# Routing seven groups ahead of the last, group-wise one-hot tables, a multiply on GpSimd and a gate column of its own, in a gated cross-attention and mixture-of-experts block

## The reference

```python
# x: 4 x 1024 x 256; ctx: 4 x 77 x 256; mask: 1 x 1024 x 77
x = x + tanh(g_xattn[0]) * xattn(layernorm(x), ctx, ctx, mask, W1, b1, W2, b2)   # softmax attention over 77 keys
h = layernorm(x).reshape(4096, 256)
route   = softmax(h @ router_w + router_b)          # 8 experts
max_ind = argmax(route); max_prob = max(route)
for e in range(8):                                   # only the chosen expert's y counts
    a, g = split(h @ w1[e])                          # 256 -> 2 x 1024
    y = silu(a) * g @ w2[e]                          # 1024 -> 256
    out = where(max_ind == e, y, out)
x = x + tanh(g_ffn[0]) * out * max_prob
```

## Time and profile before

| | us |
|---|---|
| median of 3 runs | 452.51 |
| lowest, highest | 451.57, 454.33 |
| the profiled execution | 450.66 |
| its span (first to last instruction) | 448.6 |

### The profile page before, as it was taken

One profiled execution on the slowest core, in us unless ns is written; L12 is line 12 of the kernel. 1 busy time (PEld: TensorE's weight loads), 2 busy tenths in 40 slices (PEclk: granted clock), 3 DMA queues, 4 the chain that ended last, 5 costly groups with the idle time before them and its releaser, 6 DMA issues.

```text
span 448.6 us, 9824 instructions
## 1 busy us (share of the span) xinstructions
PE 399.7 (89%) x2431; PEld 346.0 (77%) x2432; DVE 213.7 (48%) x520; ACT 175.9 (39%) x337; POOL 246.2 (55%) x323
## 2 busy tenths in 40 slices
PE   5998872149999999999999999999999999999990
PEld 4887751037888888888888888888888888888880
DVE  4888995842443443344443444433434434444340
ACT  1276650014543454545532344445433543233230
POOL 2566989020875677887773258728852676232221
PEclk9999996558999999999999999999999999999997
DMA  7951222652333044433342103433331011001010
GB/s 212 361 188 51 97 99 80 102 200 84 119 118 117 23 147 173 145 117 117 123 161 80 36 18 117 135 112 124 117 117 36 4 36 36 24 24 28 24 35 11
DMA packets 29850, 44.27 MB, mean 99 GB/s; under 512 B 8377, under 2 KB 25581, under 8 KB 27791
## 3 DMA queue, kind: packets, MB, share of 16 engines
q1 hardware_dynamic: 24095, 34.58, 23.4%
q0 software_dynamic: 3456, 9.24, 6.3%
q10 hardware_dynamic: 2288, 0.33, 0.5%
HBM read 35.57 MB, written 8.96 MB: 99 GB/s over the span
## 4 chain that ended last, share of the span: by engine, by line
PE 79%; POOL 8%; DVE 6%; DMA 2%; issue 2%; ACT 1%; DVEq 0%; SPq 0%; POOLq 0%; ACTq 0%
PE py L1093 22%; PE pa L1075 22%; PE pg L1075 21%; PE ph L1085 7%; POOL w_lo L411 2%; PE px L1060 2%; POOL rstd L395 2%; PE ps_s L1004 1%; DMA ctx_in<-in_ctx 1%; POOL slot_iota L432 1%; PE ps_p L948 1%; DMA x_sorted<-residual_rows,idx_gather 1%; DVE x_all L728 1%; PE ps_xt L920 1%; POOL mask_c L387 1%
## 5 line engine op out<-in xcount | busy, mean ns | idle before, releaser
L875 DVE TENSOR_TENSOR ht_lo<-ph,ht_hi 128x512 fp32r<-128x512 f32 x70 | 48.4, 692 | 135.9 <-ACT ht_hi L610 135.9
L481 POOL TENSOR_TENSOR w_lo<-staging,w_hi x84 | 107.4, 1307 | 6.7 <-ACT w_hi L631 4.0
L610 ACT CAST ht_hi<-ph 128x512 fp32r<-128x512 f32 x70 | 41.1, 587 | 121.3 <-PE ph L1085 86.0
L1093 PE MATMUL py<-w_hi,ht_hi 128*128 x280 | 81.3, 290 | 0.8 <-DVE out_tile L883 0.8
L1093 PE MATMUL py<-w_hi,ht_lo 128*128 x280 | 78.4, 280 | 0.0
L1093 PE MATMUL py<-w_lo,ht_hi 128*128 x280 | 78.3, 280 | 0.0
L470 POOL DMA_INDIRECT out<-out_tile,idx_now x34 | 34.7, 1019 | 72.0 <-DVE out_tile L883 71.3
L1075 PE MATMUL pa<-w_hi,xt_hi 128*128 (+1 forms) x140 | 58.8, 420 | 0.8 <-ACT xt_hi L592 0.8
L439 POOL DMA_INDIRECT x_sorted<-residual_rows,idx_now x34 | 35.6, 1048 | 40.8 <-DVE x_norm L858 22.7
L1075 PE MATMUL pg<-w_hi,xt_hi 128*128 (+1 forms) x140 | 56.1, 401 | 0.0
L1075 PE MATMUL pa<-w_lo,xt_hi 128*128 (+1 forms) x140 | 56.1, 401 | 0.0
(11 more groups left out here) (167 smaller groups left out, 577.5 us busy)
## 6 DMA issues: line engine op xcount, KB each, us to landing
staging<-in_L_ffn_w SPq DMA_DIRECT2D x24, 1024.0 KB, 4.9
residual_rows<-x_all SPq DMA_DIRECT2D x8, 532.0 KB, 3.6
x_all<-in_x SPq DMA_DIRECT2D x8, 512.0 KB, 9.9
x_sorted<-residual_rows,idx_now POOLq DMA_INDIRECT x34, 3.9
out<-out_tile,idx_now POOLq DMA_INDIRECT x34, 2.5
w_in<-in_L_xattn_W SPq DMA_DIRECT2D x2, 256.0 KB, 4.7
ctx_in<-in_ctx SPq DMA_DIRECT2D x1, 308.0 KB
mask_in<-in_fside_1xSxS ACTq DMA_DIRECT2D x1, 308.0 KB, 11.2
```

What stands on the lines that cost most here:

```text
L481: lo = nc.gpsimd.tensor_tensor(out=w_lo[:, bass.ds(dst + q * QW, QW)], in0=staging[:, bass.ds(src + q * QW, QW)], in1=w_hi[:, bass.ds(dst ...
L610: nc.scalar.copy(ht_hi[:, j], ph[j][:]).then_inc(hhi_ready[j], 1)
L875: nc.vector.tensor_tensor(out=ht_lo[:, j], in0=ph[j][:], in1=ht_hi[:, j].bitcast(FP32), op=ALU.subtract).then_inc(hlo_ready[j], 1)
L1093: last = mm(py[:, 0:D], ht[:, j, c * P:(c + 1) * P], w[:, bass.ds(slot + (DC * PW + (j * HC + c) * D), D)], start=j == 0 and n == 0, stop= ...
```

## The change

Five edits.

1. `norm2` makes the logits before it writes the two numbers of the row.
2. The routing up to `onehot` runs twice (`PARTS`): for the 28 tiles of groups 0 to 6, and for the 4 tiles of group 7. ACT's exponential is split likewise. The gates and all that follows run once, when both are done.
3. The tables shrink to one group's width (128 x 4 and 55 x 4), and the comparisons read them again for each group. `slot_hot` and `col_hot` are laid out by group, with a group's 4 tiles innermost. The one-hots are made in three rounds (`ROUNDS`) of 3, 3 and 2 groups, `col_hot` ahead of `slot_hot`; `FIRST` goes from 3 to 4, as the tables now reach into group 3, and DVE no longer waits for the other row stores.
4. The product with the token's number is made by POOL for the first round (a semaphore each way), by DVE for the others.
5. A row becomes mean x rstd, rstd, the 256 values and the gate (259 numbers instead of 266); the gate has its own column, so SP stores gates without waiting for the row stores. POOL waits for the row stores ahead of the first gather instead.

```diff
-    ROW = XW + 2
+    X0 = 2
+    XROW = X0 + XW
+    KEPT = X0 + D
+    ROW = KEPT + 1
-    HT = NT // 2
-    FIRST = 3
+    PARTS = ((0, NG - 1), (NG - 1, NG))
+    ROUNDS = ((0, 3), (3, 6), (6, NG))
+    FIRST = 4
...
-        slot_iota = sb1("slot_iota", [P, P, NT], FP16)
-        col_iota = sb1("col_iota", [P, COLS, NT], FP16)
-        slot_hot = sb1("slot_hot", [P, P, NT], FP16)
-        col_hot = sb1("col_hot", [P, COLS, NT], FP16)
+        slot_hot = sb1("slot_hot", [P, NG, P, B], FP16)
+        col_hot = sb1("col_hot", [P, NG, COLS, B], FP16)
+        slot_iota = sb1("slot_iota", [P, P, B], FP16)
+        col_iota = sb1("col_iota", [P, COLS, B], FP16)
...
# SP
             for g in range(NG):
                 sp.wait_ge(rstd2_ready, g + 1)
-                sp.dma_start(rows_groups[g], x_all[:, g]).then_inc(first_stored if g < FIRST else rows_stored, 16)
-            sp.wait_ge(first_stored, 16 * FIRST)
-            sp.wait_ge(rows_stored, 16 * (NG - FIRST))
+                sp.dma_start(rows_groups[g, :, :, 0:KEPT], x_all[:, g, :, 0:KEPT]).then_inc(first_stored if g < FIRST else rows_stored, 16)
             sp.wait_ge(gate_ready, 1)
...
# POOL, norm2
-                nc.gpsimd.tensor_copy(x_all[:, g, :, XW + 1], rstd2[:, g])
-                nc.gpsimd.tensor_tensor(out=x_all[:, g, :, XW], in0=mv2[:, r, :, 0], in1=rstd2[:, g],
-                                        op=ALU.mult).then_inc(rstd2_ready, 1)
...
                                         op=ALU.add).then_inc(logits_ready, 1)
+                nc.gpsimd.tensor_copy(x_all[:, g, :, 1], rstd2[:, g])
+                nc.gpsimd.tensor_tensor(out=x_all[:, g, :, 0], in0=mv2[:, r, :, 0], in1=rstd2[:, g],
+                                        op=ALU.mult).then_inc(rstd2_ready, 1)
...
+            end_group = ROUNDS[0][1]
+            pool.wait_ge(col_ready, 1)
+            nc.gpsimd.tensor_tensor(out=col_hot[:, 0:end_group], in0=col_hot[:, 0:end_group],
+                                    in1=token_of[:, 0:end_group].unsqueeze(2).to_broadcast([P, end_group, COLS, B]),
+                                    op=ALU.mult).then_inc(token_ready, 1)
+
+            pool.wait_ge(first_stored, 16 * FIRST)
+            pool.wait_ge(rows_stored, 16 * (NG - FIRST))
             pool.wait_ge(gate_stored, 16 * B)
             pool.wait_ge(lists_ready, 1)
...
# DVE, routing
-            dve.wait_ge(logits_ready, NG)
             dve.wait_ge(consts_ready, 4)
...
+            for part, (first_group, end_group) in enumerate(PARTS):
+                at = slice(first_group * B, end_group * B)
+                n = (end_group - first_group) * B
+                dve.wait_ge(logits_ready, end_group)
+                link(nc.vector.tensor_reduce(best[:, at], logits[:, at], AX.X, ALU.max))
...
+                nc.vector.tensor_tensor(out=onehot[:, :, at], in0=expert_m8[:].unsqueeze(2).to_broadcast([P, E, n]),
+                                        in1=first[:, at].unsqueeze(1).to_broadcast([P, E, n]),
+                                        op=ALU.is_equal).then_inc(onehot_ready, 1)
+            dve.wait_ge(onehot_ready, len(PARTS))
+            dve.wait_ge(gate_exp, len(PARTS))
...
# DVE, one-hots
             dve.wait_ge(first_stored, 16 * FIRST)
-            dve.wait_ge(rows_stored, 16 * (NG - FIRST))
...
+            for r, (first_group, end_group) in enumerate(ROUNDS):
...
+                nc.vector.tensor_tensor(out=col_hot[:, at], in0=of_group(col_iota, COLS),
+                                        in1=of_token(pos_f[:, 0], COLS), op=ALU.is_equal).then_inc(col_ready, 1)
+                slots = nc.vector.tensor_tensor(out=slot_hot[:, at], in0=of_group(slot_iota, P),
+                                                in1=of_token(pos_f[:, 1], P), op=ALU.is_equal)
+                if r == 0:
+                    slots.then_inc(hot_ready, 1)
+                else:
+                    dve.wait_ge(col_ready, r + 1)
+                    nc.vector.tensor_tensor(out=col_hot[:, at], in0=col_hot[:, at], in1=of_token(token_v[:], COLS),
+                                            op=ALU.mult).then_inc(hot_ready, 1)
...
# PE
+            for r, (first_group, end_group) in enumerate(ROUNDS):
+                if r == 0:
+                    pe.wait_ge(token_ready, 1)
+                pe.wait_ge(hot_ready, r + 1)
+                for g in range(first_group, end_group):
+                    for b in range(B):
+                        last = mm(ps_s[0][:, 0:COLS], slot_hot[:, g, :, b], col_hot[:, g, :, b],
+                                  start=g == 0 and b == 0, stop=g == NG - 1 and b == B - 1)
```

More of the change, by code:

```diff
@@ L575, in _ @@
                     high0(i)
-            act.wait_ge(centered, 1)
-            nc.scalar.activation(work_e[:], work_b[:], ACT.Exp).then_inc(gate_exp, 1)
+            for part, (first_group, end_group) in enumerate(PARTS):
+                at = slice(first_group * B, end_group * B)
+                act.wait_ge(centered, part + 1)
+                nc.scalar.activation(work_e[:, at], work_b[:, at], ACT.Exp).then_inc(gate_exp, 1)
             act.wait_ge(tab_psum, 1)
@@ L645, in stats1 @@
                 for b in range(B):
-                    last = nc.vector.bn_stats(bn1[:, g, b], x_all[:, g, b, 0:D])
+                    last = nc.vector.bn_stats(bn1[:, g, b], x_all[:, g, b, X0:KEPT])
                 last.then_inc(bn1_ready, 1)
@@ L735, in stats2 @@
                 for b in range(B):
[L736 removed]
+                    last = nc.vector.bn_stats(bn2[:, r, b], x_all[:, g, b, X0:KEPT])
                 last.then_inc(bn2_ready, 1)
@@ L777, in _ @@
[L777 to L783, removed]
@@ L784, in _ @@
-            dve.wait_ge(gate_exp, 1)
+            dve.wait_ge(consts_ready, 4)
+            for part, (first_group, end_group) in enumerate(PARTS):
+                at = slice(first_group * B, end_group * B)
+                n = (end_group - first_group) * B
+                dve.wait_ge(logits_ready, end_group)
+                link(nc.vector.tensor_reduce(best[:, at], logits[:, at], AX.X, ALU.max))
+                nc.vector.tensor_tensor(out=work_b[:, at], in0=logits[:, at],
+                                        in1=best[:, at].unsqueeze(2).to_broadcast([P, n, E]),
+                                        op=ALU.subtract).then_inc(centered, 1)
+                dve.wait_ge(centered, part + 1)
+                link(nc.vector.scalar_tensor_tensor(out=work_a[:, at], in0=work_b[:, at], scalar=0.0,
+                                                    in1=expert_m8[:].unsqueeze(1).to_broadcast([P, n, E]),
+                                                    op0=ALU.is_equal, op1=ALU.mult))
+                link(nc.vector.tensor_reduce(first[:, at], work_a[:, at], AX.X, ALU.min))
+                nc.vector.tensor_tensor(out=onehot[:, :, at], in0=expert_m8[:].unsqueeze(2).to_broadcast([P, E, n]),
+                                        in1=first[:, at].unsqueeze(1).to_broadcast([P, E, n]),
+                                        op=ALU.is_equal).then_inc(onehot_ready, 1)
@@ L815, in _, with of_group, of_token @@
             dve.wait_ge(first_stored, 16 * FIRST)
-            dve.wait_ge(rows_stored, 16 * (NG - FIRST))
[L817 to L828, removed]
+            for r, (first_group, end_group) in enumerate(ROUNDS):
+                at = slice(first_group, end_group)
+                n = end_group - first_group
+                def of_group(table, m):
+                    return table[:].unsqueeze(1).to_broadcast([P, n, m, B])
+                def of_token(v, m):
+                    return v.rearrange("p (g b) -> p g b", b=B)[:, at].unsqueeze(2).to_broadcast([P, n, m, B])
+                nc.vector.tensor_tensor(out=col_hot[:, at], in0=of_group(col_iota, COLS),
[8 more added lines that the diff above has]
+                                            op=ALU.mult).then_inc(hot_ready, 1)
             dve.wait_ge(lists_step, 1)
@@ L919, in transpose_tokens @@
                     for b in range(B):
-                        last = nc.tensor.transpose(ps_xt[k][:, b * P:(b + 1) * P], x_all[:, g, b, k * P:(k + 1) * P],
+                        last = nc.tensor.transpose(ps_xt[k][:, b * P:(b + 1) * P], x_all[:, g, b, X0 + k * P:X0 + (k + 1) * P],
                                                    ident[:])
```

39 lines of the change are left out of this document (15 added, 24 removed).

## The result

The changed kernel took 449.33 us in the median of 18 runs (447.0 to 452.5), the kernel before 452.19 in 18 runs beside it (450.6 to 455.55). The ratio is 0.9934, 95% interval 0.9909 to 0.996: 3.0 us less (1.8 to 4.1). The prediction was 449.3, in a range of 446.9 to 451.3. A second series (8 and 25 runs) gave 0.9901 (0.9862 to 0.994).

The account below looks back on a forecast made before the run. TensorE bounds the loop, which can only start earlier. A gain of 3.6 us before the one-hots less 0.3 there, taken as 3.2, gave 450.66 - 3.2 = 447.4; the median lies 1.85 above: 449.3, range 446.9 to 451.3.

Parts of the forecast that it names:

- The one-hots: Comparisons, products and list matmuls: VectorE held by POOL's 1.6 us product, matmuls at 0.123 us each; a loss of 0.3 us.
- a step put at nothing: First gather: comes earlier along with SP's weight loads, its length changed only by 3% through shorter rows.
- The tables and the lateness of POOL: Before the routing: smaller tables take 0.83 us, covered by 4.8 us until group 7's statistics, so POOL is no longer late.
- Seven groups first: Routing up to onehot: part 0 hides behind norm2(7), part 1 takes 1.13 us; onehot is complete 3.84 us earlier.
- term of 0.2 us for collisions: Routing part 0 beside norm2(7): POOL's short operations hold DVE up by 0.2 us, between bounds of 0 and 1.1.
- Rival B: In norm2(7), POOL's power function also holds DVE: 1.0 us less, gain 2.2, 450.3 us; chance 0.11.
- From O to T: From onehot complete to the first comparison of the one-hots: the 5.06 us in between stay unchanged.
- Rival A: One-hots: DVE and POOL don't exclude each other; stage gains 0.7 us, 448.0 us in all; chance 0.22.
- D: One-hots: POOL's product is slow; at 4.9 us the whole gain is gone, at 9.4 the time is 457; chance 0.09.
- What costs nothing: Gate stores, row stores, moved waits, weight loads, shorter rows: nothing lost; gates land by 86.3, with 4.4 us of cover.
- The clock: Start of the loop: full clock back near 101 us, with the first up matmul at 97.0; before, 4.2 us after it.
- rival C: Start of the loop: the clock rises at the same moment as before, 104.4; gain 1.6 us, 450.9 us; chance 0.08.

Follow-up runs that it names:

- one-part kernel: Changed kernel with all 32 tiles routed in one part instead of seven groups ahead; 450.64 us, ratio 0.9935 to the kernel before.
- same kernel with quarters: Changed kernel with all products on VectorE, rounds of 4, 3 and 1 groups, GpSimd's weight subtractions in quarters, not eighths; 449.39 us, ratio 0.9919 to the kernel before.

## Why the prediction was right

The direction was right, and the first two steps for the reason given. The time came out to 0.03 us, and that is luck: the one-hots gained 1.06 us more than forecast, the first gather took 0.2 to 1.8 back, a step put at nothing, and the interval of the measured gain alone is 2.3 us wide.

**The tables and the lateness of POOL.** Right: POOL waits 1.77 us for group 7's statistics instead of being 2.5 late, and S to O is 3.50 for a predicted 3.46 (3.26 and 0.2 of charge). Wrong in its price: the tables took 1.21 and 0.58 us, 2.4 and 2.6 ns a number and not 1.0. It stayed hidden, but not under the 4.8 us of cover that I counted: `norm2(6)`, 2.27 us, lies in them, and 1.77 were left. And the 7.09 us that this step starts from belong to one execution; the second profile of before has 6.56, against which the step gains 0.5 less.

**Seven groups first.** The term of 0.2 us for collisions was right in sum and wrong in its side. I had DVE wait for POOL; DVE's operations took their 0.39, and POOL was held, its power function 1.19 and the next 0.40. The logits came at S + 2.39 instead of 2.06, and DVE, done with part 0, waited 0.46. The one-part kernel shows the 0.31 us as what DVE's presence costs. Rival B, a power function that holds DVE for 1.0, is out: an operation with two inputs in SBUF, begun at 77.53, ran in 0.39 us inside POOL's power function (77.19 to 78.38).

**From O to T.** Missed by 0.12: DVE now waits for `onehot` to be complete where it ran on before.

**The one-hots.** The mechanism was right: POOL's product got its turn right after the slot comparison and held the next comparison, 1.59 us for 0.50. Rival A is out. Mis-sized were two terms. The product was taken as 1.6 us in working time; alone it takes 1.29, and between DVE's operations 1.15 (from the slot comparison's end at 86.85). The matmuls were left at 0.123 each; they take 0.068, as the layout by group brings their numbers together. A loss of 0.33 was forecast, 0.71 was gained (6.73 to 6.02). Of the 1.06 between, 0.46 is the product (DVE is done at T + 5.36 and not 5.82) and 0.60 the matmuls. I named faster matmuls only under rival A, and there for the weights, which make the smaller part; they belonged into the forecast with a chance of their own. D, a slow product, did not come: 2.0 ns a number.

**What costs nothing.** Right for the gates (the run with SP's waits back); the waits of POOL and the row format were not varied by themselves. Wrong for the first gather: I wrote that the loads come earlier "with the gather" and left its 3.61 us as it stood. It took 3.99 and 5.34 in the two profiles of the changed kernel, 3.61 and 3.85 before. So L to U gave back 0.2 to 1.8 us. The 1.06 us that the one-hots gained beyond the forecast went there, in part or in whole.

**The clock.** The sum took it to come back at the same distance from the first up matmul, 4.2 us. In the first profile of the changed kernel that was 3.75 us (at 102.5), in the second 5.9, and in the second of before 5.9 as well; over the 14 profiles it is 2.9 to 5.9, at 100.3 to 107.5. So neither the forecast's fixed distance nor rival C's fixed moment holds; what sets it isn't shown, and it alone moves the time by up to 1.4 us (half of 3.0, roughly). The granted clock by stretch in the changed kernel (from:to, length, busy us of PE, PEld, DVE, ACT, POOL, clock, DMA):

```profile
99.00:102.00 3.00, 3.00 (x8) 2.35 (x9) 0.06 (x1) 0.90 (x1) 0.36 (x1) 0.50 0.51 128
102.00:103.00 1.00, 1.00 (x5) 0.82 (x4) 0.00 (x0) 0.00 (x0) 0.00 (x0) 0.78 1.07 376
103.00:106.00 3.00, 3.00 (x14) 2.42 (x14) 1.01 (x2) 0.89 (x2) 0.10 (x1) 1.00 0.41 143
```

**The account of the two first profiles.** The spans differ by 0.9 us (448.6, 447.7). S came 2.26 later; 1.59 of that the second profile of before has too, and variants with the change lie at 74.5 to 75.0. S to U gained 3.77. The third `x_norm` cost 1.27 more, which also occurs before (1.99 in its second profile); the earlier clock and the rest give back 0.66. The forecast of 3.2 for the change is to be set against 3.77 and, with the long gather, 2.2 to 2.4 in the stretch, and 3.0 (1.8 to 4.1) in the medians.

## What to carry to other kernels

Shrink what stands in front of a late engine before splitting the work behind it: small tables, read again by an access pattern, gave 2.9 to 3.4 us together with the layout that they bring, routing ahead 0.9. Work handed to a second engine is free only if the two don't hold each other; here POOL's product cost 0.7 us more than leaving it where it was. And when a stretch gets shorter, look at which transfer its first DMA now meets.

## What the runs showed of the hardware that I had not expected

- A VectorE instruction that waits for GpSimd doesn't always get the next gap. Beside subtractions of 1.3 us `x_norm` waited through one or, once in an execution, two (at most 1.99 us, in either kernel). Beside pieces of 0.7 us 17 of 21 went at the next gap or at once, and three waited through all that were left (3.5 us); the median was 15 us above that of the same kernel with quarters.
- The step of the moving operand counts most in the pace of small float16 matmuls at the half clock: 55 numbers 8 bytes apart 0.068 us a matmul, 64 bytes apart 0.111, with the weights at 8 bytes in both; weights 64 bytes apart add 0.014.
- GpSimd's tables in runs of 4 cost 2.4 ns a number (512 in 1.21 us), in runs of 32 1.0 (4096 in 4.15).
- DVE's float16 comparisons kept their rate with runs of 4 repeated numbers: 1536 in 0.87 us, 0.57 ns a number, where the float32 rows have 1.05.
